# Building the adjacency of a graph network: two tiles at fixed slots and then one tile a turn, instead of one tile and then pairs, in blocks 9 to 24

## The reference, cut to what matters

```python
src = randint(0, 3125, (100000,))
dst = minimum(int(3125 * uniform ** 2), 49999)      # many edges go to low nodes
order = argsort(dst)                                # edges sorted by dst
src, dst = src[order], dst[order]

# layer 0, both ways: sums of h weighted by edge_weight, divided by the sum of weights
msum = segment_sum(h[src] * w[:, None], dst); wsum = segment_sum(w, dst)
# layer 1 (three hops) and layer 2 (four orders): unweighted or weighted sums over the same edges
Y = segment_sum(edge_weight[:, None] * X[src], dst)
agg = segment_sum(x[src], dst) * deg_inv
```

## Time and profile before

| | us |
|---|---|
| median of three runs | 3447.63 (3442.16 to 3459.87) |
| the profiled execution | 3462.01 |
| its span | 3460.3 |
| of this, blocks 9 to 24 (from one L822 to another) | 467.33 |
| PE, DVE, ACT, POOL busy over the whole span | 3101.3, 1641.2, 1243.1, 880.0 |

### The profile page before, as it was taken

How to read it: one execution, slowest core, us unless ns; L and a number is a source line. 1 busy time by engine, 2 the same in 40 slices (tenths; PEclk the granted TensorE clock), 3 DMA queues, 4 the chain that set the end, 5 groups by cost and what they waited for, 6 DMA issues and landing times. The chain is left out here.

```text
span 3460.3 us, 84662 instructions
## 1 busy us (share of the span) xinstructions
PE 3101.3 (90%) x24442; PEld 2425.7 (70%) x24443; DVE 1641.2 (47%) x4485; ACT 1243.1 (36%) x3783; POOL 880.0 (25%) x938
## 2 busy tenths in 40 slices
PE   5999998999988999999789999999996788888887
PEld 3677676667764444444479999999885677777777
DVE  7988778889974310000544211111234455554454
ACT  6777777777731220000433222111243111111111
POOL 2000000000020000000167777200123766655640
PEclk8999999999999999999689999999997899999999
DMA  3011222333359287979035323222342444444431
GB/s 88 12 62 63 85 91 92 111 102 120 127 142 232 51 197 188 235 178 216 12 93 129 102 74 83 74 74 73 99 118 68 108 104 102 103 100 96 102 88 64
DMA packets 115789, 368.41 MB, mean 106 GB/s; under 512 B 37613, under 2 KB 54481, under 8 KB 102712
## 3 DMA queue, kind: packets, MB, share of 16 engines
q1 hardware_dynamic: 86647, 334.12, 35.1%
q0 software_dynamic: 25696, 29.21, 5.6%
q10 hardware_dynamic: 3154, 1.60, 0.2%
HBM read 278.22 MB, written 86.61 MB: 105 GB/s over the span
## 5 line engine op out<-in xcount | busy, mean ns | idle before, releaser
L2670 POOL DMA_INDIRECT edge_rows<-src_table,src_idx x432 | 443.3, 1026 | 251.4 <-issue 121.6
L2312 POOL DMA_INDIRECT slots<-lane,src_idx x352 | 342.9, 974 | 107.6 <-issue 107.6
L798 ACT ACTIVATE build_place<-build_place,w 128x128 f32<-128x128 bf16 x770 | 290.2, 402 | 144.5 <-DVE build_place L740 103.1
L868 PE MATMUL build_ps<-build_place 128*128 128x325 bf16 (+1 forms) x1540 | 334.0, 299 | 2.7 <-ACT build_place L798 1.5
L1439 PE MATMUL prop_ps<-rows,y 125*128 125x500 f32 (+1 forms) x798 | 307.4, 544 | 15.8 <-DMA rows<-adj_rows 8.8
L860 PE MATMUL build_ps<-build_place 128*128 128x300 bf16 (+1 forms) x770 | 231.7, 301 | 66.5 <-DVE build_place L742 39.4
L740 DVE TENSOR_SCALAR build_place<-key_id,lane,one_w 128x128 f32<-128x128 f16 x770 | 262.4, 341 | 56.7 <-issue 30.0
L742 DVE TENSOR_SCALAR build_place<-key_id,key,win_base 128x300 bf16<-128x300 f16 (+1 forms) x770 | 275.0, 357 | 1.0 <-issue 0.4
L1439 PEld LDWEIGHTS prop_ps<-rows,y 125*128 125x128 f32 x798 | 143.9, 192 | 177.3 <-issue 154.4
L2863 PE MATMUL edge_ps<-edge_work 128*128 x2128 | 262.4, 278 | 2.0
L2863 PEld LDWEIGHTS edge_ps<-edge_work 128*128 128x128 f32 x2128 | 247.7, 192 | 7.9 <-issue 6.1
(11 more groups left out here) (466 smaller groups left out, 6111.7 us busy)
## 6 DMA issues: line engine op xcount, KB each, us to landing
rows<-adj_rows SPq DMA_DIRECT2D x62, 1367.2 KB
cnt_panels<-build_cnt SPq DMA_DIRECT2D x50, 683.6 KB
adj_rows<-rows SPq DMA_DIRECT2D x25, 1367.2 KB
n<-cnt_panels SPq DMA_DIRECT2D x40, 683.6 KB
orders_panel<-cnt_panels SPq DMA_DIRECT2D x40, 683.6 KB
edge_src_row<-slot_lanes SPq DMA_DIRECT2D x60, 250.0 KB
edge_dst_row<-slot_dst SPq DMA_DIRECT2D x60, 250.0 KB
h<-cnt_panels SPq DMA_DIRECT2D x20, 683.6 KB
```

What stands on the lines that cost most here:

```text
L798: a.activation(places[s].wide(r, Places.SCALED), places[s].narrow(r, Places.LANES, 1), ACT.Copy, scale=g.w12[:, bass.ds(t, 1)]).then_inc(s ...
L868: last = pe.matmul(ps[:, weight_bank(j), 0:KW[j % 2]], places[s].narrow(r, Places.SCALED, i), moving, start=False, stop=False, skip_group_ ...
L2312: pool.indirect_dma_start(dr.slots, bass.IndirectOffsetOnAxis(ap=g.src_idx[:, j:j + 1], axis=0), g.pay[:, j, :], None).then_inc(s_scattere ...
L2670: pool.indirect_dma_start(rows[:, r % AHEAD, i, :], None, dr.table, bass.IndirectOffsetOnAxis(ap=g.src_idx[:, t:t + 1], axis=0)).then_inc( ...
```

## The change

The form PAIR is replaced by SINGLE in blocks 9 to 24. A window now has tile 0 in slot 5q, a second tile in slot 5q + 1 (under the semaphores of slot 12 + q, as SHARED has it), both ahead of what `after_first` and the load do, and then a loop of n - 1 turns with one tile each, always in slot 5q + 2. That is n + 1 tiles: 3 for n = 2 as before, and 4 for n = 3 where there were 5. The number of turns is 1 for n = 2 and 2 for n = 3, before and after. Over blocks 9 to 24 there are 514 tiles before and 497 after. A wait that stood once per block and side for the handover from SHARED falls away.

```diff
@@ -516,7 +516,7 @@
         last.then_inc(self.s_done[1], 1)
 
 
-PAIR, QUAD, SHARED = 2, 4, 3
+PAIR, QUAD, SHARED, SINGLE = 2, 4, 3, 1
 SECOND = 9
 ROWS_KEPT = 5
 SLOT_OF = [2, 1] * 4 + [4, 0, 1, 2, 0, 1, 2, 3] * 2 + [4]
@@ -535,27 +535,32 @@
     def tiles(self, d, j, parity, how, one):
         i = (j if parity else j + 2) % 4
         both = self.eng.snap(self.regs[i], min_val=0, max_val=NT * RANGE)
-        step = QUAD if how == QUAD else PAIR
+        step = {QUAD: QUAD, SHARED: PAIR, SINGLE: 1}[how]
         self.eng.reg_mov(self.now[0], both >> RANGE_BITS)
         if how == SHARED:
             self.eng.reg_mov(self.now[1], (both >> RANGE_BITS) + (both & (RANGE - PAIR)) + 2)
+        elif how == SINGLE:
+            self.eng.reg_mov(self.now[1], (both >> RANGE_BITS) + (both & (RANGE - 1)) + 1)
         else:
             self.eng.reg_mov(self.now[1], (both >> RANGE_BITS) + ((both + (step - 1)) & (RANGE - step)) + 1)
         lo, end = (self.eng.snap(r, min_val=0, max_val=NT - QUAD) for r in self.now)
         one(0, lo, d * (WPB // 2) + (j // 2 + 1), None)
-        if how == SHARED:
+        if how != QUAD:
             one(SECOND, lo + 1, d * (WPB // 2) + (j // 2 + 1 - WPB // 2), None)
         if i == 3:
             self.eng.load(self.regs, self.g.spans[0:1, bass.ds(d * WPB + (j + 3), 4)])
-        with self.eng.Fori(lo + (2 if how == SHARED else 1), end, step) as t:
+        with self.eng.Fori(lo + (1 if how == QUAD else 2), end, step) as t:
             if how == SHARED:
                 n, at = self.ring.next()
                 one(1, t, n, at)
                 one(2, t + 1, n, at)
             else:
                 n = self.turns[j % 2].next()
-                for k in range(step):
-                    one(1 + k, t + k if k else t, n, None)
+                if how == SINGLE:
+                    one(2, t, n, None)
+                else:
+                    for k in range(step):
+                        one(1 + k, t + k if k else t, n, None)
 
 
 class Counts:
@@ -572,11 +577,11 @@
         turn = j if parity in (None, 1) else j + WPB
         both = self.eng.snap(self.regs[turn // 2 % 4], min_val=0, max_val=NT * RANGE)
         n = both & (RANGE - 1) if turn % 2 else both >> RANGE_BITS
-        self.eng.reg_mov(self.now, (n + 3) >> 2 if how == QUAD else n >> 1 if how == SHARED else (n + 1) >> 1)
+        self.eng.reg_mov(self.now, (n + 3) >> 2 if how == QUAD else n >> 1 if how == SHARED else n - 1)
         turns = self.eng.snap(self.now, min_val=1, max_val=NT)
         before_first()
         one(0, d * (WPB // 2) + (j // 2 + 1), None)
-        if how == SHARED:
+        if how != QUAD:
             one(SECOND, d * (WPB // 2) + (j // 2 + 1 - WPB // 2), None)
         if parity is None and turn in (7, 9):
             self.eng.load(self.regs, self.g.counts[0:1, 4:8] if turn == 7 else self.g.counts[0:1, 8:12])
@@ -590,8 +595,11 @@
                 one(2, n, at)
             else:
                 n = self.turns[j % 2].next()
-                for k in range(QUAD if how == QUAD else PAIR):
-                    one(1 + k, n, None)
+                if how == SINGLE:
+                    one(2, n, None)
+                else:
+                    for k in range(QUAD):
+                        one(1 + k, n, None)
         after_last()
 
 
@@ -707,7 +715,7 @@
 
         def blocks(eng, block_of):
             block_of(0, None, 0, QUAD, None)
-            for first, last, pairs, how in ((0, PAIRS, 1, SHARED), (1, NB // 2 // PAIRS, PAIRS, PAIR)):
+            for first, last, pairs, how in ((0, PAIRS, 1, SHARED), (1, NB // 2 // PAIRS, PAIRS, SINGLE)):
                 with eng.Fori(first, last) as turn:
                     for i in range(2 * pairs):
                         f = first * 2 * pairs + i
@@ -729,11 +737,11 @@
             spans = Spans(v, g, Ring(v, DEPTH))
             v.tensor_scalar(minus[:], g.ident[:], -1.0, None, ALU.mult).then_inc(s_minus, 1)
 
-            def one(q, e):
+            def one(q, e, how):
                 def tile(place, t, n, r):
                     at = bass.ds(t, 1)
                     s = place_of(q, place, r)
-                    if place == SECOND:
+                    if place == SECOND and how == SHARED:
 
                         v.wait_ge(s_free[5 * q + 1], v.snap(spans.turns[q].now() + 1))
                     v.wait_ge(s_free[s], n)
@@ -761,10 +769,8 @@
             def block_of(d, parity, pair, how, slot):
                 for j in range(WPB):
                     e = d * (WPB // 2) + j // 2
-                    if how == PAIR and j < 2:
-                        v.wait_ge(s_free[SLOTS + j], PAIRS * 2 * (WPB // 2) + 1)
-                    spans.tiles(d, j, parity, how, one(j % 2, e))
-                    if parity is not None and how == PAIR:
+                    spans.tiles(d, j, parity, how, one(j % 2, e, how))
+                    if parity is not None and how == SINGLE:
                         low(d * WPB + j - 2, *before(d, j, parity, 2)[:2])
                     if parity is not None:
                         if 1 <= j <= NG and j - 1 in MOVES[0]:
@@ -832,7 +838,7 @@
                     if j or parity is not None:
                         jb, pb, db = before(d, j, parity, 1)
                         out_of_psum(w - 1, jb, pb, db if parity is not None else None, pair)
-                    if (j >= 2 or parity is not None) and how != PAIR:
+                    if (j >= 2 or parity is not None) and how != SINGLE:
                         low(w - 2, *before(d, j, parity, 2)[:2])
                     if parity is not None:
                         if 1 <= j <= NG and j - 1 in MOVES[1]:
```

## The result

The changed kernel takes 3460.99 us (median of 19 runs, 3451.92 to 3474.00) against 3449.08 us before (19 runs, 3437.38 to 3460.49). The ratio is 1.0033 with a 95% interval of 1.0022 to 1.0044: a difference of 11.9 us. The interval doesn't reach 1, so the kernel is slower, by less than the 0.5% that the prediction called no change. One of the ten runs of the kernel before in its repetition further down took 7926.61 us, for a reason that stays open, and is left out of its ratio.

A forecast was written before the change was run, and what follows sets the result against it. PE and DVE were taken to bound blocks 9 to 24 in turns. Tiles -0.3, transposes +10.9 and loads -4.2 summed to +6.4 us on the 3447.6 us median: 3454 us, within 0.5%, range 3438 to 3469.

The forecast's parts named there:

- Seventeen tiles fewer: Windows with n = 3: the removed tile lay in the shadow of a slot wait; gain 0.3 us, bounds 0 and 15.2.
- The bound of the slope: Windows with n = 3: block 9 against block 16 gives 0.89 us a tile, 15.2 us gained in all.
- Transposes one tile later: j = 1 to 7: DVE's copies at j = 3 and 7 come 0.55 us later; loss 10.9 us, bounds 0 and 14.3.
- 0.24 is absorbed and 0.31 is lost: j = 3: DVE's lead over PE absorbs part of each copy's 0.55 us delay; 14 copies lose 4.3 us.
- the upper bound for 26 copies: j = 3 and 7: every one of 26 copies loses its full 0.55 us, 14.3 us in all.
- Load and branch: j = 9 of eight even blocks: a second tile covers DVE's load; gain 8 x 0.53 = 4.2 us, bounds 0 and 4.2.
- PE has waited 1.07 us for it: j = 9 in an even block: PE waits for DVE's tile 1, which starts 0.66 us late behind load and branch.
- The small things at 0: Loop turns cost the same; ACT's branch behind the second tile costs at most 1.6 us, taken as 0; handover wait long met.
- The slope: Rival, windows with n = 3: each gives back 0.89 us; 3428 us with load gain and free transposes; chance 0.07.
- The absorbed case: Rival, DVE's copies: PE's backlog hides the later transposes, no change, 3443 us; chance 0.22.
- The single slot as a new bound: Rival, windows with n = 3: each loses 0.57 us; +25.6, 3473 us; chance 0.14 together with a near relative.
- The Trainium skill's rule on recurring gaps: Slot waits, n = 3: recurring gaps can mean too few buffers; applied here, up to 9.7 us lost, sum +16.4.

The follow-up runs named there:

- the kernel with both ahead: Changed kernel with transposes and register loads ahead of the second tile again; 465.59 us in blocks 9 to 24, ratio 0.9998 to the kernel before.
- the transposes ahead: Changed kernel with PE's transposes ahead of the second tile again, loads still behind it; 464.16 us in blocks 9 to 24, ratio 0.9979 to the kernel before.

## Why the prediction came out as it did

**The forecast**, 3454 us, within 0.5%, range 3438 to 3469, held: 3460.99. The working said +6.4 us, and +11.9 was measured (+12.6 in the sixteen blocks). That the time fell in the range says little of the terms: any sum between -17 and +17 us was called no change. The terms were off by 4.7, 2.9 and -1.4 us, and the last partly made up for the first two.

**Seventeen tiles fewer: 0.3 us forecast, 1.7 measured,** with a scatter of 1. The argument that the new last tile waits for its slot as long as the old last tile took was right to the detail: 17 waits, 29.6 us for a forecast of 29. The bound of the slope, 15.2 us, was refuted by the kernel with both ahead.

**Transposes one tile later: 10.9 us forecast, 15.6 measured.** The mechanism was right, and so was the count: 26 waits, 32.8 us for 26 to 30. The step that failed is the size: "0.24 is absorbed and 0.31 is lost" at j = 3, and nothing for ACT's groups. DVE's two groups alone cost 14.3 us, as much as the upper bound for 26 copies, and all groups 15.6. In blocks 18 to 24 j = 3 and 4 together lose 0.45 us on PE: 0.29 to 0.36 as forecast in j = 3, and then 0.09 to 0.16 in the second tile of j = 4, where PE waits for ACT's half. Windows 7 and 8 lose 0.54 to 0.62 for a forecast of 0.55. Another 0.20 us appears at j = 5 of even blocks; 0.14 of it comes with ACT's groups placed late, which cost 1.4 us in sum. It is one of the windows with a register load on all three engines; why ACT's late groups cost something there and nothing at j = 1, 2, 4 and 6 stays open.

**Load and branch: 4.2 us forecast, 1.3 measured.** The step "PE has waited 1.07 us for it" took the list's word that PE waited for DVE. PE and ACT had loads of their own there, and all three moved back together: PE's load of 1232 ns in that window became one of 968 behind the second tile, and the tile behind it still came 0.89 us late. DVE's gap fell to 0.37 to 0.40 us in six of the eight even blocks and 0.65 and 0.73 in the others, not to near 0.1, and it wasn't the last to end. With the transposes ahead, the later load makes j = 9 of the even blocks 0.35 us longer and j = 0 of the odd ones 0.34 shorter, so the place that was to give the 4.2 us gives nothing; what is gained is 0.15 us at j = 5 of the even blocks, where the prediction took nothing (with the transposes late, 0.65 us at j = 3 of the odd ones).

**The small things at 0** were not tested alone. ACT's 1.53 us before its third tile at j = 9 look large, but it had stood 1.30 us before its second tile there before the change; whatever that adds is inside the measured 1.3.

**The single blocks.** Block 9 was forecast within 1 us of 36.21 and took 36.67. Block 19 was forecast at 27.3 us and took 26.49, and block 16 at 27.6 and took 29.11: the later L828 of the even blocks moves time from odd blocks to even ones, which the forecast left out. The sixteen took 479.89 us for 474.

**The rivals.** The slope is out. The absorbed case is out: L725's wait doubled instead of staying at 16. The single slot as a new bound is out too, as the 17 windows got no longer: on PE they add up to 74.7 us before and 74.2 after. The Trainium skill's rule on recurring gaps (Perfetto Trace Analysis, Optimization Strategy) named a real shortage: without the slot's wait each of these windows is 1.2 to 1.7 us shorter. But the change didn't make the windows longer, and the cost came from elsewhere.

## What to carry to other kernels

When a piece of code is moved behind another on one engine, look for who waits for it on another: here 0.55 us of PE's order cost about as much behind each of 26 copies on DVE, 14.3 us, where the seventeen tiles saved were worth 1.7. Removing work from a loop gains little where the new last step waits for a buffer that is released by the same chain, and a test of that is to compute when that step can start. A buffer chosen by a register can take its wait away and cost more than it in the register's work: here 10.1 us. And where an engine is said to wait for another, see whether it had a register load of its own at that moment.

## What the runs showed of the hardware

- At j = 9 of every even block (10 to 24) the register loads of all three engines are slow: before the change 1077 to 1296 ns on DVE, 1023 to 1188 on ACT and 992 to 1541 on PE, with medians over blocks 9 to 24 of 346, 312 and 334. At j = 3 of most odd blocks DVE's and ACT's are slow as well (the longest, 1765 ns, is one of these), though PE loads nothing there. What makes them slow stays open.
- Block 17 took 33.23 and 32.94 us in the two profiles at a granted clock of 0.90, though block 18 had 27.30 and 29.35 at 1.00. It is the first block of the outer loop's second turn. At its start PE stood idle for 3.24 us in the profile before, behind the outer loop's branch, which took 3447 ns once and 216 in the median; then the granted clock was 0.56 and 0.70 on the mean, and 1.00 again from 760 us on:

```profile
L711 PEldq COMPARE_BRANCH  x6: 73/216/3447, 264.2 to 969.3; - x6
```

```profile
750.00:753.00 3.00, 1.56 (x7) 0.97 (x8) 2.71 (x9) 2.10 (x7) 0.00 (x0) 0.56 0.05 14
753.00:760.00 7.00, 7.00 (x42) 5.27 (x41) 6.22 (x21) 4.50 (x14) 0.00 (x0) 0.70 0.65 214
```

- Two chips ran the kernel before some 720 us slower. Blocks 9 to 24 were not touched; the stage with POOL's indirect transfers was. The kernel with the transposes ahead on such a chip, and the kernel before on the first one, from 1600 to 2300 us:

```profile
1600.00:2300.00 700.00, 230.14 (x1709) 171.78 (x1708) 103.28 (x303) 92.77 (x425) 367.01 (x355) 0.62 0.13 31
```

```profile
1600.00:2300.00 700.00, 662.70 (x5943) 588.24 (x5942) 193.16 (x616) 200.24 (x828) 352.07 (x355) 0.95 0.35 89
```

POOL has 355 instructions in either stretch and is busy 367 us for 352. But PE is busy 230 us there for 663, at a mean clock of 0.62 for 0.95, and the DMA moves 31 GB/s for 89. What is different about those chips stays open.
